# Fused attention kernel: the text queries of a unit's eight heads packed into five tiles of 128 rows

## The reference

```python
qkv = hidden_states @ Wqkv                      # 32 query heads of 32, one key, one value head
scores = einsum('bqhd,bkd->bhqk', q, k) * 32**-0.5 + alibi     # causal
probs = softmax(scores)
h = h + (einsum('bhqk,bkd->bqhd', probs, v).reshape(B, S, H)) @ Wo
h = h + ffn(layernorm(h))                       # base matmul plus eight routed low-rank experts
```

## Time and profile before

| | |
|---|---|
| median of 3 runs | 1572.31 us (1569.68 to 1573.06) |
| the profiled execution: its time, its span | 1572.91 us, 1571.1 us |
| mean granted TensorE clock | 0.987 |
| busy share of the span: PE, PEld, DVE, ACT, POOL | 94%, 83%, 68%, 47%, 32% |
| attention with its projections | from about 139 us to about 900 us of the span |
| values of the 64 units | first at 199.2 us, last at 897.8 us |

### The profile page before, as it was taken

The page is one execution under the profiler, slowest core; times in us unless marked ns, Lnnn a source line. Parts: engine busy times, 40 slices in busy tenths (PEclk is TensorE's granted clock), DMA queues, the critical chain, the costliest instruction groups (busy, mean ns, idle before and its releaser), DMA issues. The chain is left out here.

```text
span 1571.1 us, 28985 instructions
## 1 busy us (share of the span) xinstructions
PE 1479.0 (94%) x9796; PEld 1311.3 (83%) x9796; DVE 1071.4 (68%) x4158; ACT 742.8 (47%) x2557; POOL 507.4 (32%) x317
## 2 busy tenths in 40 slices
PE   3894999999999999999999989999999999999999
PEld 2784988888888888888887769898989898999898
DVE  7887688888979888897988565353534444444464
ACT  6693586868878786877888431111111111010001
POOL 0001465757475665757544301010101010101010
PEclk9997999999999999999999999999999999999999
DMA  9865754554656364554775251212121212121211
GB/s 307 290 141 123 114 111 87 77 114 66 130 87 120 64 119 83 79 116 71 154 157 113 76 190 47 75 40 80 40 80 40 80 40 80 40 80 40 71 49 41
DMA packets 107646, 153.63 MB, mean 98 GB/s; under 512 B 8948, under 2 KB 93300, under 8 KB 106600
## 3 DMA queue, kind: packets, MB, share of 16 engines
q1 hardware_dynamic: 106712, 151.78, 41.5%
q10 hardware_dynamic: 816, 0.39, 0.1%
HBM read 75.00 MB, written 51.38 MB: 80 GB/s over the span
## 5 line engine op out<-in xcount | busy, mean ns | idle before, releaser
L954 ACT ACTIVATE P<-P,nmax 128x128 f32<-128x128 f32 (+1 forms) x1024 | 434.4, 426 | 91.5 <-DVE nmax L1063 87.4
L1038 POOL TENSOR_TENSOR P<-P,rden 128x512 f32<-128x512 f32 (+1 forms) x256 | 331.9, 1318 | 269.4 <-DVE rden L1069 269.1
L1063 DVE CUSTOM_DVE_ANT_0 P<-sc,mask 128x128 f32<-128x128 f32 (+1 forms) x1024 | 292.7, 323 | 77.2 <-PE sc L829 71.2
L1440 POOL TENSOR_TENSOR ht<-ht 128x1024 f32<-128x1024 f32 (+1 forms) x24 | 58.1, 2422 | 575.5 <-DVE ht L1469 575.5
L859 PE MATMUL pr<-xT_hi,wq_hi 128*128 128x410 f32 x576 | 242.6, 421 | 0.5 <-DVE xT_lo L1090 0.5
L1075 DVE COPY PTR<-pt 128x282 f32<-128x282 f32 x512 | 221.0, 432 | 27.4 <-PE pt L839 26.4
L1337 PE MATMUL b<-w_hi,x2T_hi 128*128 128x390 f32 (+3 forms) x624 | 214.5, 344 | 1.0 <-DVE x2T_lo L1484 1.0
L1337 PE MATMUL b<-w_lo,x2T_hi 128*128 128x390 f32 (+3 forms) x624 | 212.5, 341 | 0.0
L1337 PE MATMUL b<-w_hi,x2T_lo 128*128 128x390 f32 (+3 forms) x624 | 212.0, 340 | 0.0
L859 PE MATMUL pr<-xT_lo,wq_hi 128*128 128x410 f32 x576 | 201.4, 350 | 0.0
L859 PE MATMUL pr<-xT_hi,wq_lo 128*128 128x410 f32 x576 | 200.2, 348 | 0.0
(11 more groups left out here) (212 smaller groups left out, 2931.3 us busy)
## 6 DMA issues: line engine op xcount, KB each, us to landing
Qs<-q_hi SPq DMA_DIRECT2D x128, 205.0 KB, 4.8
ht<-h_dram SPq DMA_DIRECT2D x42, 512.0 KB, 3.7
Qs<-q_lo SPq DMA_DIRECT2D x64, 205.0 KB, 5.7
att_dram<-att SPq DMA_DIRECT2D x64, 205.0 KB, 3.0
at<-att_dram SPq DMA_DIRECT2D x25, 512.0 KB, 4.9
out<-ht SPq DMA_DIRECT2D x23, 512.0 KB, 2.7
h_dram<-Y SPq DMA_DIRECT2D x61, 128.0 KB, 3.2
h_dram<-in_txt SPq DMA_DIRECT2D x1, 4928.0 KB, 40.7
```

What stands on the lines that cost most here:

```text
L954: last = nc.scalar.activation(P[rows, j % 2, i, cols], P[rows, j % 2, i, cols], ACT.Exp, scale=-1.0, bias=nmax[at], accum_out=den[at])
L1038: lastp = nc.gpsimd.tensor_tensor(w, w, r, ALU.mult)
L1063: lastv = v.tensor_tensor_reduce(P[0:n, j % 2, i, cols], sc[i % 2][0:n, cols], mask[0:n, m], 1.0, 3.0e38, ALU.add, ALU.min, nmax[0:n, j % ...
L1440: nc.gpsimd.tensor_tensor(rows(t, par)[0:n, :], rows(t, par)[0:n, :], base_b[0:n, :], ALU.add).then_inc(biased, 1)
```

## The change

The image queries keep their eight multiplications, maxima, exponentials and turns of 128 rows. The text queries of a unit (8 heads of 77 rows, 616) are laid side by side in a new buffer `Qt`, head by head, by one copy on ACT (`pack_text`, in step 5 of the slot before the unit's scores), and are then worked on as five tiles of 128, 128, 128, 128 and 104 rows, in steps 0, 2, 3, 5 and 6. Each tile has its own mask, maximum, exponential and turn. PE waits for the packing (`text_packed`) before a unit's first scores. `values` becomes three groups of multiplications: V of the image keys for the 256 image columns, then for the 154 text columns, then V of the text keys for these. POOL's instruction for the text covers three tiles in the first half, two in the second. `crow` is laid over a part of the new buffer `PTI`, and `mask` grows to 1153 columns. The diff, cut to its core:

```diff
+TEXT_ROWS = GH * TXT
+PACKS = [(f, min(128, TEXT_ROWS - f)) for f in range(0, TEXT_ROWS, 128)]
+PACK_STEP = [0, 2, 3, 5, 6]
+MASK_COLS = CH + len(PACKS) * S
...
+    Qt = sb("Qt", [128, 2, TEXT_ROWS], F32R)
+    P, Pt = sb("P", [128, 2, GH, CH]), sb("Pt", [128, 2, len(PACKS), S])
+    HALF_PACKS = [[k for k, at in enumerate(PACK_STEP) if at // 4 == half] for half in range(2)]
+    PTI, PTT = sb("PTI", [128, 2, GH, CH]), sb("PTT", [128, 2, 2, TEXT_ROWS])
+    crow = PTI[:, 1].rearrange("p h t -> p (h t)")[:, 0:16 + 4 * (S + 1)]
...
+    PACK_TEXT_AT = 5
...
+    def next_unit(p, slot, first, last):
+        found = att_unit(slot, -1)
+        if found is None or (found[0] and first) or (not found[0] and last is None):
+            return None
+        return p - found[0], found[1]
...
+                    pe.wait_ge(text_packed, 8 * p + j + 1)
...
-                nc.tensor.matmul(bank[:, 0:CH], q[:, 0:CH], Ks[0:QR, g // 2, b, 0:CH], start=True, stop=True)
-                nc.tensor.matmul(bank[0:TXT, CH:CH + S + 1], q[:, CH:S], Ks[0:QR, g // 2, b, :],
-                                 start=True, stop=True).then_inc(scores_done, 1)
+                lasts = nc.tensor.matmul(bank[:, 0:CH], q[:, 0:CH], Ks[0:QR, g // 2, b, 0:CH], start=True, stop=True)
+                k = pack_of(i)
+                if k is not None:
+                    f, n = PACKS[k]
+                    lasts = nc.tensor.matmul(bank[0:n, CH:CH + S + 1], Qt[0:QR, b, f:f + n], Ks[0:QR, g // 2, b, :], start=True, stop=True)
+                lasts.then_inc(scores_done, 1)
...
-                nc.tensor.transpose(bank[:, 0:CH], src[:, 0:CH], ident[:])
-                nc.tensor.transpose(bank[:, CH:S], src[0:TXT, CH:2 * CH], ident[0:TXT, 0:TXT])
-                nc.tensor.transpose(bank[0:TXT, S:S + TXT], src[0:TXT, 2 * CH:CH + S],
-                                    ident[0:TXT, 0:TXT]).then_inc(transposed, 1)
+                lastt = nc.tensor.transpose(bank[:, 0:CH], P[:, j % 2, i, :], ident[:])
+                k = pack_of(i)
+                if k is not None:
+                    n, src = PACKS[k][1], Pt[:, j % 2, k, :]
+                    nc.tensor.transpose(bank[:, CH:CH + n], src[0:n, 0:CH], ident[0:n, 0:n])
+                    lastt = nc.tensor.transpose(bank[0:TXT, 2 * CH:2 * CH + n], src[0:n, CH:S], ident[0:n, 0:n])
+                lastt.then_inc(transposed, 1)
...
-                    nc.tensor.matmul(o[rows, 0:2 * S], V0[:, b, :], PT0[:, j % 2, q:q + 5:4, :], start=True, stop=False)
+                    nc.tensor.matmul(out[:, :, 0:CH], V0[:, b, :], PTI[:, j % 2, q:q + 5:4, :], start=True, stop=True)
...
+                    nc.tensor.matmul(out[:, :, CH:S], V0[:, b, :], PTT[:, j % 2, 0].rearrange("p (h t) -> p h t", t=TXT)[:, q:q + 5:4, :],
+                                     start=True, stop=False)
...
+            def pack_text(p, j):
+                g, b = j // 2, j % 2
+                for q in q_stacked:
+                    act.wait_ge(q, 16 * STACKS * (4 * p + g + 1))
+                if p + j == 0:
+                    act.wait_ge(rows_ready, 3)
+                wait_count(act, scores_done, 64 * p + 8 * (j - 1))
+                nc.scalar.activation(Qt[0:QR, b].rearrange("p (h t) -> p h t", t=TXT), Qs[0:QR, g % 2, :, b * S + CH:(b + 1) * S].bitcast(F32),
+                                     ACT.Copy).then_inc(text_packed, 1)
...
                         if sj is not None:
                             exp_head(*sj, i)
+                        if i == PACK_TEXT_AT and next_unit(p, slot, first, last) is not None:
+                            pack_text(*next_unit(p, slot, first, last))
...
-                v.tensor_copy(PTR[:, j % 2, i, :], pt[i % 2][:, 0:S + TXT]).then_inc(pT_copied, 1)
+                lastc = v.tensor_copy(PTI[:, j % 2, i, :], pt[i % 2][:, 0:CH])
+                k = pack_of(i)
+                if k is not None:
+                    f, n = PACKS[k]
+                    lastc = v.tensor_copy(PTT[:, j % 2, :, f:f + n], pt[i % 2][:, CH:3 * CH].rearrange("p (c t) -> p c t", c=2)[:, :, 0:n])
+                lastc.then_inc(pT_copied, 1)
```

More of the change, by code:

```diff
@@ L716, in slots, with pack_of, columns @@
             yield slot, (MAIN[slot] if last is not None else None), unit(0), unit(1), unit(2)
+    def next_unit(p, slot, first, last):
[3 more added lines that the diff above has]
+        return p - found[0], found[1]
+    def pack_of(i):
+        return PACK_STEP.index(i) if i in PACK_STEP else None
+    def columns(j, i):
+        half, k = i // 4, pack_of(i)
+        return (j % 2, half, slice(i % 4, i % 4 + 1)), None if k is None else (j % 2, half, slice(4 + k - HALF_PACKS[half][0], 5 + k - HALF_PACKS[half][0]))
     with nc.Block() as block:
@@ L951, in exp_head @@
                 act.wait_ge(scores_biased, 64 * p + 8 * j + i + 1)
-                for t, (rows, cols) in enumerate(((slice(0, CH), slice(0, CH)), (slice(0, TXT), slice(CH, CH + S)))):
-                    at = (rows, j % 2, i // 4, t, slice(i % 4, i % 4 + 1))
-                    last = nc.scalar.activation(P[rows, j % 2, i, cols], P[rows, j % 2, i, cols], ACT.Exp, scale=-1.0,
-                                                bias=nmax[at], accum_out=den[at])
-                last.then_inc(exp_done, 1)
+                head, pack = columns(j, i)
+                rows = [(CH, P[:, j % 2, i, :], head)]
+                if pack is not None:
+                    rows.append((PACKS[pack_of(i)][1], Pt[:, j % 2, pack_of(i), :], pack))
+                for n, x, at in rows:
+                    at = (slice(0, n),) + at
+                    last = nc.scalar.activation(x[0:n], x[0:n], ACT.Exp, scale=-1.0, bias=nmax[at], accum_out=den[at])
+                last.then_inc(exp_done, 1)
+            def pack_text(p, j):
[7 more added lines that the diff above has]
+                                     ACT.Copy).then_inc(text_packed, 1)
             def a_hi(t):
@@ L1591, in constants @@
         rows[2 * late:2 * late + 2, 16:] = both.reshape(-1)
-    k, p = np.arange(256)[None, :] - 128, np.arange(128)[:, None]
+    masks = np.zeros((128, MASK_COLS), f)
+    masks[:, 0:CH] = np.where(np.arange(CH)[None, :] > np.arange(CH)[:, None], f(1e30), f(0))
+    for pack, (first, n) in enumerate(PACKS):
+        own = (first + np.arange(n)) % TXT
+        at = CH + pack * S + CH
+        masks[0:n, at:at + TXT] = np.where(np.arange(TXT)[None, :] > own[:, None], f(1e30), f(0))
     steps, coarse = np.zeros((2, 64, HCH, 128), f), np.zeros((2, 64, 2, HCH, AH), f)
@@ L1608, in constants @@
         "ident": np.eye(128, dtype=f),
-        "mask": np.where(k > p, f(1e30), f(0)).astype(f),
+        "mask": masks,
         "rows": rows,
```

46 lines of the change are left out of this document (26 added, 20 removed).

## The result

Four runs of the changed kernel have a median of 1529.38 us (1528.62 to 1531.54), four runs of the kernel before beside them 1571.73: a ratio of 0.9734 (95% interval 0.9717 to 0.9751), **42 us less**, twice the gain forecast and outside the range. The profiled execution took 1528.77 us with a span of 1527.0.

What follows compares the result with a forecast made beforehand. Most of a pair was taken as PE's own stream, a quarter as DVE's, plus one small POOL stall. PE −18, DVE −3, POOL −3, lateness +3 sum to −21 us: 1551 against the median of 1572.3, range 1538 to 1569.

Steps and rivals of the forecast that it cites:

- "−3" for DVE: Two statistics slots of a pair, where DVE sets the pace: 0.5 us comes off instead of 0.28, −3 us in all.
- "−3" for POOL: PE's 0.8 us stall behind POOL once a pair: covered by smaller text tiles, half taken back by PE's earlier arrival, −3 us.
- "+3" for lateness: Charge for occasional lateness of ACT's packing before the first scores and for DVE's uneven steps: +3 us.
- 2 × 0.2 × 7 pairs: DVE's gain beyond PE's own in two statistics slots of each of seven pairs, 0.2 us each: −3 us in all.
- −0.28 us per unit: PE's net saving per unit, −0.31 in the steps plus 0.03 for one more hand-over in the values; × 64 = −18 us.
- image score 0.10 (the turn's 128 columns load behind it): PE step without text: the image score costs 0.10 us because the turn's weight load sets it; step 0.77 to 0.78 against 1.02.
- The values: Values of a unit on PE, in three groups: 1.09 us as before plus one more hand-over of 0.03, about 1.1 us.
- the steps with a packed score: PE's steps with a packed text score: the score adds 0.105 us; a step with packed score and turns takes 1.10.
- the mask's load: Start: the mask grows to 590 KB, loading in 6.2 us within 9.0 us of cover, costing nothing; at most 3 us otherwise.
- "more": Rival, 11%: streaming alone prices PE's scores, gain 0.6 per unit where PE leads, DVE holds the statistics slots; 1541 us.
- "Half the gain": Rival, 20%: DVE's and ACT's latency replaces PE's time, PE gives back 10 of its 18 us; 1561 us.
- "slower": Rival, 11%: DVE becomes the bound in heavy steps, each of thirteen copies carrying 0.14 fixed; +11 us, 1583.

Runs made afterwards that it cites:

- b_recip: Kernel before, with nine of the ten links of the layer norm's rstd chain as one-input reciprocals, so rstd is not computed; ratio 0.9969, pair 88.3 us.
- b_pool: Kernel before, with POOL's text multiplication cut from 205 to 128 columns per head, 77 text keys left undivided; 1558.33 us, ratio 0.9929.
- b_dve: Kernel before, with DVE's copy of a turned head cut from 282 to 220 elements, turned text keys left out; 1565.35 us, ratio 0.9967.
- b_imagelast: Kernel before, with the turn of the image square after those of the text instead of first; 1563.07 us, ratio 0.9951.
- b_dve_pool: Kernel before, with both DVE's copy cut to 220 elements and POOL's text multiplication cut to 128 columns; 1553.38 us, ratio 0.9890.
- a_pool: Changed kernel, with an extra POOL multiplication of 110 or 310 columns ahead of each half, giving POOL its old time; 1546.97 us, ratio 0.9850.

## Why the prediction was wrong

Two terms failed, by about 11 us each: the relief of DVE and POOL, nearly five times what was written, and PE's own saving.

**The step that failed most** is the relief of DVE and POOL. The prediction gave "−3" for DVE, "−3" for POOL and charged "+3" for lateness: −3 us together over seven pairs, 0.4 a pair. In the kernel before both reliefs together were worth 2.7 a pair. Taken back in the changed one they cost 2.5 and 0.4, with POOL's by far the larger.

- **POOL, the term most wrong.** The prediction looked for POOL's price where the waits name POOL: one stall of 0.8. It took half of it; the whole of it came (17.61 to 16.77). And somewhat more lay in waits that the profile puts down to DVE: the two-input links that stood behind POOL, 0.74 and 0.79 us long where the same instructions otherwise take 0.15, in two slots where PE waits for DVE. b_recip, which leaves POOL's work as it was, takes 1.1 us off the pair in just the two slots where b_pool takes 1.0 of its 1.9. POOL's two text instructions themselves shrank by 1.0 us per unit, not by 1.2.
- **DVE.** "2 × 0.2 × 7 pairs", taken as what the statistics slots gain beyond PE's own saving. b_dve gives 0.4 and 0.3 in these slots and 0.1 each in two more: 0.9 a pair by itself. The prediction netted it against PE's saving, but in a slot that DVE paces, PE's saving isn't there to be netted: b_imagelast shortened PE's stream by 0.3 per unit and these slots by 0.04. The prices were right: the copies are 0.20 and 0.33 apart (412.60 to 412.80 and 411.63 to 411.96 in the changed kernel's timeline of DVE), with durations of 275 and 413 ns, and the start-to-start reading of the earlier trace rows held against the Trainium skill's fixed 120 cycles ("VectorE: DVE Perf Modes", section on the TRN2 errata), by which DVE would have gained too little to matter.
- **The charge of +3** wasn't needed: PE waits 0.7 us for the packing in all. The risk was real: two steps later it is +71 us.

**PE, direction right, size off.** Forecast −0.28 us per unit, measured 9.00 − 9.45 = −0.45. The failed sub-step is "image score 0.10 (the turn's 128 columns load behind it)": it is 0.06. A step without packed pieces does not occur (each of the eight has one or both), but taking two turns of 0.11 from 0.95 leaves 0.73, not 0.775: 8 × 0.045 = 0.36 more. On the other side the packed score costs 0.145 and not 0.105, 0.2 back. Net −0.17 per unit, 11 us in 64 units. The Trainium skill's rule ("TensorE: Matmul & The Clock Gate", section LDWEIGHTS) that a weight load takes its column count over 1.2 GHz fits the packed score: 51 columns more are 0.043 us by it, and the stretch from the text score to the turn grew from 0.10 to 0.145. It does not fit the turns: by it 128 columns need 107 ns, and 0.06 were enough here and in b_imagelast. The prediction had one price for both kinds, and it booked the 0.10 ahead of the turn in the earlier trace rows to the turn's weights. With the same turn behind it this stretch grew when the text score's own weights did, so I read it as the score's. Why a turn's load hides and a score's doesn't stays open.

**The sum again, with the measured terms.** A pair was forecast 2.7 shorter (86.7) and is 5.8 shorter. PE: 8 × 0.45 = 3.6, reliefs 2.7, together 6.3. The table of slots shows where the missing 0.5 is: from b_dve_pool to the changed kernel the two statistics slots lose 0.22 and 0.18 (10.55 to 10.33, 9.91 to 9.73) and not 0.45 each. That there only one of the two savings counts is argued from it. For the whole program, PE gives 64 × 0.45 = 29 us. Beyond PE's 3.6 each of the first six pairs gives 2.2; the last two, which have no statistics, give 0.7 and 0.2 (start times of the values): 14 in all, against the 3 of the forecast. So PE is 11 us over its forecast of 18 and the rest 11 over its 3, and these 22 are the measured excess (1551 less 1529.4).

**What held.** The values (1.09, forecast 1.1), the packing (713 ns, forecast 740), POOL's text instructions (1253 and 873 ns, forecast 1.2 and 0.8), the steps with a packed score (0.89 alone and 1.09 with turns; forecast 0.88 and 1.10; the step with turns alone is 0.95, not 1.00), and the mask's load, whose cover kept: the first values start at 194.8 us, with the mixer 3.9 earlier, against 199.2. **The rivals:** "more" had 1541 by another mechanism (streaming alone) that held for the turns' loads and not for the scores', and it too stopped at DVE. Its own terms give more than it says: 0.6 for 0.3 per unit is 0.3 × 48 = 14 us and not 0.2 × 48, so 1537. "Half the gain" and "slower", both on DVE as the new bound, were ruled out by a DVE that got 0.5 us per unit lighter. The case that came, all terms and POOL's hidden part, wasn't among them.

## What to carry to other kernels

Where an engine paces a slot, look for its instructions that last much longer than others of their shape, and compare their ends with those of POOL: here two-input DVE links beside long POOL instructions were paid for on DVE's path and booked to DVE. Whether that costs time is another question: in the changed kernel such links still stood, and taking the stand away gave nothing. Price a saving by the slot: what PE saves counts only where PE leads, what DVE saves only where DVE leads, and the netting is to be done slot by slot. A price for a short PE instruction holds for the kind of its successor (score, turn or main), so it is read from the same succession, or bounded from both sides.

## What the runs showed of the hardware that was not expected

- Links on 128 × 4 elements with two inputs last up to 0.79 us instead of 0.15, and then end within 0.03 us of a running POOL instruction's end; as reciprocals, with one input, they take 0.17 beside it. A one-input tensor_scalar on an int32 view stands all the same, up to 0.88 us in a_pool.
- A turn with 128 weight columns starts 0.06 us behind a short instruction. Behind a score that streams 206 columns the next instruction starts after 0.145 us where the score has 128 weight columns, and after 0.10 where it has 77. In the profile the image turn's weight load has a mean of 140 ns and the image score's 189, both of 128 columns.
- A turn costs by the columns that it streams, not by the weight columns of the next: 0.11 us for 128 (387.35 to 387.46, ahead of a turn with 77 weight columns), 0.09 for 104 (388.45 to 388.54 in the changed kernel), 0.06 for 77 (398.72 to 398.78 in b_imagelast, ahead of one with 128).
